# Perceiver decoder: attention weights, contexts and row statistics prepared in the feed-forward's program

## The chip, the cores and the metric

The kernel runs on 1 core of one Trainium2 chip. The metric is the device time of one execution in microseconds (us), as the median of 3 runs. The engines are PE (matrix engine; PEld is its weight load), DVE (vector), ACT (scalar, activation functions), POOL (GpSimd) and SP, which issues the DMA transfers.

## The reference, cut to what matters

Six residual blocks are applied in turn to x (32 batches x 64 positions x 256). The change touches the third and the fourth.

```
x = x + L0_xattn(ctx_1024, layernorm(x), ...)     # program "latent_attention"
x = x + L0_attn(layernorm(x), ...)                # program "linear_feed", linear attention
x = x + L0_ffn(layernorm(x), ...)                 # program "linear_feed", gate/up/down with silu
x = x + L1_xattn(layernorm(x), ctx_1024, ...)     # "decoder": cross attention, 16 heads of 16
x = x + L1_attn(layernorm(x), ...)                # "decoder": gated cell over 64 positions
x = x + L1_ffn(layernorm(x), ...)                 # "decoder": 8 experts, entmax gates

def _L1_xattn_ref(query, key, value, mask, Wq, bq, Wk, bk, Wv, bv, Wo, bo):
    Q, K, V = query @ Wq.T + bq, key @ Wk.T + bk, value @ Wv.T + bv      # split into heads
    energy = where(mask == 0, -1e20, einsum(Q, K) / sqrt(16))
    return (softmax(energy) @ V) @ Wo.T + bo
```

## The kernel before, in words

The 2048 rows of x stay in on-chip memory as `x_sb`, in NT = 16 tiles of 128 rows; NCH = 4 chunks of PER = 4 tiles. Three programs run one after the other. Each is one block in which every engine has its own fixed list of instructions, ordered by hand, and counting semaphores between them; at a program's end (`end_stage`) the semaphores are cleared and all engines meet at a barrier. Nothing crosses that barrier but what lies in memory.

**`linear_feed`** (names `body_...` in the trace). For each chunk c, PE runs five turns i = 0..4 that mix three things: the gate and up products of the chunk before (`gate_up(c-1, i)`), and `contexts`, `states` and `keys_values` of the linear attention of this chunk's tiles. DVE does in a turn `hidden(c-1, i)` (silu times up, line 571), `contexts` (518 to 528), `states` (508, 510), `keys_values` (497, 498) and `y_row` (bn_stats of one tile, 113). At i = 4 comes `norm_y.close`, seven small operations (120 to 128), then POOL's power (137), then `scale_rows`. ACT's next copies of transposed rows (`rows_turned`, line 420), which PE's `queries` (294) wait for, come in its list behind `high(c-1, 5)` (460), which waits for DVE's `hidden(c-1, 5)`. POOL's list is `hidden_low` (line 256, the low part of each hidden block for the three-pass products), with the power for each chunk between hidden_low 3 and 4. `down` (367) waits for all six hidden_low. After chunk 3 there is no next chunk to turn, so PE goes from gate_up(2, 5) straight to `down(2, 0)`. A tail follows: hidden(3, 0..5), with gate_up alone on PE, then down(3, 0..3).

**`decoder`** (names `dec_`, `att_`, `moe_`). Its opening, in front of the loop over the 32 batches, loads the query, key and value weights and the first context (256 keys of 2 batches, transposed, `ctx_raw`), splits weights and context into a high part in fp32r and a low remainder, computes the layer-norm statistics of all 16 tiles (`rows_stats`: four bn_stats and the seven small operations; POOL's power), applies them (`rows_apply`, 140), transposes the rows on PE (`turn_rows`, 901), has ACT copy them out (1106), and multiplies by Wq (`queries`, 910, two products of 128x512 per half). `keys_proj(0)` and `values_proj(0)` are three-pass products (line 83). ACT writes one half of the scaled queries `q_bd` (1112) and DVE the other (1258); the loop's first `energies(0)` (942) waits for the last of them. The first exponentials of the loop are at line 1128.

`TileStats` holds statistics of a norm; `goes_on(stats, rstd, first)` lets a later program go on with tiles that an earlier one began, as `Ahead` does for the linear attention.

```
            turn_rows(0)
            turn_rows(1)
            pe.wait_ge(q_loads, 32)
            queries(0)
            pe.wait_ge(pre, 2)
            keys_proj(0)
            turn_rows(2)
            queries(1)
            values_proj(0)
            turn_rows(3)
            queries(2)
            queries(3)
```

## Time and profile before

| | |
|---|---|
| median of 3 runs | 2220.39 us (2218.87 to 2220.65) |
| the profiled execution | 2218.44 us, its span 2216.6 us |
| PE, PEld busy | 96%, 85% of the span |
| DVE, ACT, POOL busy | 55%, 52%, 23% |
| mean granted PE clock | 0.985 |
| `linear_feed` in the span | about 903 to 1113 us |
| opening of the decoder | 1113.8 us to the first energies at 1151.2 us |

The timeline's times are from the span's start. A row gives start, duration of the group, engine, line, operation, what it writes and reads, the count, and in brackets how long the engine idled before it and what released it.

### The profile page before, as it was taken

The numbers are of one execution on the slowest core, as the hardware profiler recorded it, in microseconds if no ns is written. First come the engines' busy times: TensorE is split into PE (matmuls) and PEld (weight loads), VectorE is DVE, ScalarE is ACT, GpSimd is POOL, SyncE is SP. The second block draws the span as 40 slices with busy tenths as digits, with TensorE's granted clock in tenths as the row PEclk, the third lists the DMA queues.
The fourth block names the chain that finished last, engine by engine and source line by source line (L and its number), as shares of the span: only waits on it lengthen the run. The fifth ranks groups of instructions, "written<-read, shape, count | busy, mean of one in ns | idle before, by whom it ended". The sixth has DMA issues, their size and how long they took to land.

```text
span 2216.6 us, 50712 instructions
## 1 busy us (share of the span) xinstructions
PE 2118.9 (96%) x20881; PEld 1883.0 (85%) x20881; DVE 1218.3 (55%) x3619; ACT 1157.9 (52%) x2620; POOL 502.8 (23%) x416
## 2 busy tenths in 40 slices
PE   6999999999999999699879999999999999999999
PEld 5899999998989998466758878878999999999998
DVE  5656565656555555657556777842874843342411
ACT  4656565656565555333237766653444444444443
POOL 0000011000000000122221221232444444444444
PEclk9999999999999999999989999998999999999999
DMA  4000200000000000000031100010101101011000
GB/s 143 21 16 21 72 21 16 23 15 28 18 18 20 16 6 1 11 1 1 1 116 31 31 26 27 12 40 1 58 1 39 39 1 39 1 39 38 1 10 29
DMA packets 48803, 58.08 MB, mean 26 GB/s; under 512 B 6528, under 2 KB 40128, under 8 KB 48448
## 3 DMA queue, kind: packets, MB, share of 16 engines
q1 hardware_dynamic: 48576, 54.85, 7.8%
q8 instruction: 167, 2.74, 0.5%
q14 instruction: 60, 0.49, 0.1%
HBM read 46.72 MB, written 2.10 MB: 22 GB/s over the span
## 4 chain that ended last, share of the span: by engine, by line
PE 45%; DVE 3%; issue 1%; ACT 1%; POOL 0%; POOLq 0%; DVEq 0%; ACTq 0%
PE bank L83 20%; PE bank L1031 16%; PE bank L969 3%; PE bank L955 2%; PE bank L942 1%; PE bank L910 1%; PE bank L978 1%; PE bank L997 1%; DVE dec_room L140 0%; DVE att_rden L1290 0%; DVE att_vz L1272 0%; PE bank L1002 0%; DVE dec_ts_rawa L113 0%; PE bank L901 0%; PE bank L990 0%
## 5 line engine op out<-in xcount | busy, mean ns | idle before, releaser
L861 POOL TENSOR_TENSOR moe_h<-moe_hr,moe_h 128x512 fp32r<-128x512 f32 x256 | 340.8, 1331 | 431.3 <-ACT moe_hr L1175 431.3
L1174 ACT ACTIVATE moe_h<-bank,dec_b 128x512 fp32r<-128x512 f32 x256 | 176.4, 689 | 401.5 <-PE bank L83 378.0
L83 PE MATMUL bank<-lat_wv,lat_kv_t 128*128 128x256 f32 (+1 forms) x1728 | 261.9, 301 | 8.7 <-DVE lat_wv L2188 4.9
L83 PE MATMUL bank<-lat_kv_t,lat_qk 128*128 128x320 f32 x1536 | 258.8, 317 | 0.0
L83 PEld LDWEIGHTS bank<-lat_wv,lat_kv_t 128*128 128x128 f32 x1728 | 224.4, 190 | 16.8 <-ACT lat_v L2096 5.7
L83 PEld LDWEIGHTS bank<-lat_kv_t,lat_qk 128*128 128x128 f32 x1536 | 225.2, 188 | 8.7
L2121 ACT ACTIVATE lat_p<-bank,lat_neg_max 128x320 f32<-128x320 f32 x256 | 135.2, 528 | 166.2 <-DVE lat_neg_max L2237 166.2
L2231 DVE TENSOR_TENSOR lat_qk<-bank,lat_qk 128x256 fp32r<-128x256 f32 x256 | 96.7, 420 | 197.6 <-ACT lat_qk L2115 197.4
L83 PE MATMUL bank<-dec_xt,dec_lo 128*128 128x512 f32 x512 | 202.5, 396 | 0.0
L2237 DVE TENSOR_REDUCE lat_neg_max<-bank 128x1 f32<-128x320 f32 x256 | 125.7, 492 | 132.3 <-PE bank L83 132.1
L1175 ACT ACTIVATE moe_hr<-bank,dec_b 128x512 f32<-128x512 f32 x256 | 174.6, 682 | 0.0
L1652 POOL TENSOR_TENSOR lat_rs_rstdc<-lat_rs_varc,lat_rs_halfc 128x4 f32<-128x4 f32 x16 | 16.2, 1015 | 692.4 <-DVE lat_rs_varc L1644 692.4
L1031 PE MATMUL bank<-dec_hi,moe_h 128*128 128x256 f32 x1024 | 164.0, 282 | 0.4 <-POOL moe_h L861 0.4
L1031 PE MATMUL bank<-dec_lo,moe_h 128*128 128x256 f32 x1024 | 163.8, 282 | 0.0
L1031 PE MATMUL bank<-moe_hi,moe_h 128*128 128x256 f32 x1024 | 163.2, 282 | 0.4 <-POOL moe_h L861 0.4
L83 PE MATMUL bank<-dec_xt,dec_hi 128*128 128x512 f32 x512 | 162.9, 400 | 0.0
L83 PE MATMUL bank<-dec_xt,moe_hi 128*128 128x512 f32 x512 | 159.4, 392 | 0.0
L1031 PEld LDWEIGHTS bank<-dec_hi,moe_h 128*128 128x128 f32 x1024 | 149.1, 190 | 11.4 <-POOL moe_h L861 0.8
L1128 ACT ACTIVATE att_p<-att_sc,att_low 128x256 f32<-128x256 f32 x256 | 113.2, 510 | 85.6 <-DVE att_low L1282 85.6
L1031 PEld LDWEIGHTS bank<-moe_hi,moe_h 128*128 128x128 f32 x1024 | 148.6, 189 | 10.8 <-POOL moe_h L861 0.6
L1031 PEld LDWEIGHTS bank<-dec_lo,moe_h 128*128 128x128 f32 x1024 | 139.6, 189 | 0.0
L1549 DVE SCALAR_TENSOR_TENSOR x_sb<-bank,moe_xs,x_sb 128x256 f32<-128x256 f32 x96 | 41.3, 473 | 145.2 <-PE bank L1031 145.2
(321 smaller groups left out, 4060.3 us busy)
## 6 DMA issues: line engine op xcount, KB each, us to landing
raw_w<-in_L_ffn_W SPq DMA_DIRECT2D x16, 1024.0 KB, 6.4
lat_ctx_raw<-in_ctx SPq DMA_DIRECT2D x16, 512.0 KB, 4.0
att_ctx_raw<-in_ctx_turned SPq DMA_DIRECT2D x16, 512.0 KB, 3.7
lat_kv_t<-lat_lt SPq DMA_DIRECT2D x32, 128.0 KB, 2.1
out_x<-x_sb SPq DMA_DIRECT2D x4, 512.0 KB, 2.9
x_sb<-in_x SPq DMA_DIRECT2D x1, 1792.0 KB, 14.7
lat_xl_now<-lat_xl SPq DMA_DIRECT2D x7, 256.0 KB, 4.5
ahead_room<-in_L_xattn_Wq SPq DMA_DIRECT2D x1, 1024.0 KB, 7.3
```

Source lines behind the costliest of these rows:

```text
L83: mm = pe.matmul(out, lhs(a, k), rhs(b, k), start=first and k == 0 and n == 0, stop=last and k == KD - 1 and n == 2)
L861: pool.tensor_tensor(h[:, g % 2, 1, :], hr[:, g % 2, :], h[:, g % 2, 0, :].bitcast(F32), ALU.subtract).then_inc(h_lo, 1)
L955: mm = pe.transpose(pt_bank[half][:, (2 * n + t) * P:(2 * n + t + 1) * P], p[:, m, 2 * half + n, t * P:(t + 1) * P], k.ident[:, :])
L969: mm = pe.matmul(o_bank[r * W32:(r + 1) * W32, (2 * what + m) * S:(2 * what + m + 1) * S], of, pt[:, m, r, t, par * S:(par + 1) * S], star ...
L1031: mm = pe.matmul(y_bank[c % 2 * 2 + i // 2][:, i % 2 * D:(i % 2 + 1) * D], h[:, n % 2, b, i * P:(i + 1) * P], w2(e % 2, a)[:, at, :], star ...
L1128: act.activation(p[:, m, r, :], sc[:, m, r, :], ACT.Exp, bias=low[:, m, r:r + 1], scale=-1.0).then_inc(p_ready, 1)
L1174: act.activation(h[:, n % 2, 0, :], h_bank[n % 2][:, :], ACT.Relu, bias=bias).then_inc(h_hi, 1)
L1175: act.activation(hr[:, n % 2, :], h_bank[n % 2][:, :], ACT.Relu, bias=bias).then_inc(h_f, 1)
L1549: dve.scalar_tensor_tensor(out=x_sb[:, t, :], in0=src(t), scalar=xs[:, t, e:e + 1], in1=x_sb[:, t, :], op0=ALU.mult, op1=ALU.add).then_inc ...
L2121: act.activation(p[:, hp % 2, h * LK:(h + 1) * LK], s_bank[h][:, 0:LK], ACT.Exp, bias=neg_max[:, u:u + 1], accum_out=rsum[:, u:u + 1]).the ...
L2231: dve.tensor_tensor(cols(1), bank[:, 0:KD * P].rearrange("p (k b n) -> p k b n", k=KD, b=2), cols(0).bitcast(F32), ALU.subtract).then_inc( ...
L2237: dve.tensor_reduce(neg_max[:, u:u + 1], s_bank[h][:, 0:LK], AX.X, ALU.max, negate=True).then_inc(s_max, 1)
```

## The change

A class `Near` holds, for the cross attention, context buffers, Wq, Wk, Wv, the biases bq and bk and the row statistics in memory that lives from `linear_feed` into the decoder (on the right side of the memory, by `RightSide`; the buffers `h` and `hr` of the experts take that place later). In `linear_feed`, SP issues seven more loads (two biases, three weights, two contexts); DVE splits Wk and Wv (turns (1,1) and (1,2)) and the first context (turns (2,1) and (3,1)), and takes statistics of the finished chunks 0, 1 and 2 (turns (2,2) and (2,3), (3,2) and (3,3), and in the tail after hidden 2 and 3); POOL computes their power. ACT makes a silu on one column in chunk 0, so that its table is loaded there. In the decoder's opening these steps are gone; PE starts with `keys_proj(0)`; ACT starts with an exponential on one column; POOL clears `vz` after the rows of three chunks are applied; a few constants for the gated cell are made after batch 2 of the loop, not ahead of it.

```diff
+class Near:
+    CHUNKS = 3
...
+        self.ctx_raw = sb("ctx_raw", [P, 2, KD, 2 * S2])
+        self.ctx_t = sb("ctx_t", [P, 2, 2, KD, 2 * S2], F32R)
+        self.wq, self.wk, self.wv = sb("wq", [P, KD, D]), sb("wk", [P, 2, KD, D], F32R), sb("wv", [P, 2, KD, D], F32R)
...
 linear_feed, SP:
+                sp.dma_start(near.bq[:, :], column(w["L1_xattn_bq"])).then_inc(near_in, 16)
+                sp.dma_start(near.bk[:, :], column(w["L1_xattn_bk"])).then_inc(near_in, 16)
+            sp.dma_start(near.wq[:, :, :], rows(w["L1_xattn_Wq"])).then_inc(near_in, 16)
+            for g, n in enumerate(("k", "v")):
+                sp.dma_start(kv_raw[:, g], rows(w["L1_xattn_W" + n])).then_inc(near_in, 16)
+            for i in range(2):
+                sp.dma_start(near.ctx_raw[:, i], ...).then_inc(near_in, 16)
 linear_feed, POOL:
+                if c >= 2:
+                    near.norm.power(pool, c - 2)
                 norm_y.power(pool, c)
...
+                if h == 3:
+                    near.norm.power(pool, NCH - 2)
 linear_feed, ACT:
+                    if c == 0 and i == 1:
+                        act.wait_ge(l_xn, 1)
+                        act.activation(table[:, :], xn[:, 0, 0, 0:1], ACT.Silu)
 linear_feed, DVE:
+            def near_split(c, i):
+                if (c, i) == (1, 1):
+                    dve.wait_ge(near_in, 112)
+                    for g, dst in enumerate((near.wk, near.wv)):
+                        dve.tensor_copy(dst[:, 0], kv_raw[:, g]).then_inc(near_hi, 1)
+                if (c, i) == (1, 2):
...
+                        dve.tensor_tensor(dst[:, 1], kv_raw[:, g], dst[:, 0].bitcast(F32), ALU.subtract)...
+                if (c, i) == (2, 1):
+                    dve.tensor_copy(near.ctx_t[:, 0, 0], near.ctx_raw[:, 0]).then_inc(near_hi, 1)
+                if (c, i) == (3, 1):
...
+                    dve.tensor_tensor(near.ctx_t[:, 0, 1], near.ctx_raw[:, 0], ..., ALU.subtract)...
...
+                    if i == 2 and c >= 2:
+                        near_rows(c - 2)
+                    if i == 3 and c >= 2:
+                        near.norm.close(dve, c - 2)
+                    near_split(c, i)
...
+                if h == 2:
+                    near_rows(NCH - 2)
+                if h == 3:
+                    near.norm.close(dve, NCH - 2)
 decoder, PE:
+            keys_proj(0)
             turn_rows(0)
             turn_rows(1)
-            pe.wait_ge(q_loads, 32)
             queries(0)
-            pe.wait_ge(pre, 2)
-            keys_proj(0)
+            values_proj(0)
             turn_rows(2)
             queries(1)
-            values_proj(0)
             turn_rows(3)
 decoder, ACT:
+            act.activation(table[:, :], bk[:, 0:1], ACT.Exp)
+            keys_proj(0)
             rows_turned(0)
-            act.wait_ge(kv_loads, 48)
-            act.copy(wk[:, 0], wkr).then_inc(w_hi, 1)
-            act.copy(wv[:, 0], wvr).then_inc(w_hi, 1)
             rows_turned(1)
             act.wait_ge(pre, 1)
             queries(0)
-            keys_proj(0)
...
-            act.wait_ge(r_const, 5)
             for b in range(B):
+                if b == 4:
+                    act.wait_ge(r_const, 4)
 decoder, DVE:
+            rows_apply(0)
...
-            rows_stats(0)
-            rows_stats(1)
-            rows_apply(0)
-            rows_stats(2)
-            rows_apply(1)
...
-            split_keys(0)
...
+            rows_apply(1)
+            rows_apply(2)
+            rows_stats(3)
             queries(0)
-            rows_stats(3)
-            rows_apply(2)
+            rows_apply(3)
             dve.wait_ge(loads, 96)
-            s.give(dve.tensor_scalar(mask[:, :], mask_i, 0.0, MASKED, ALU.is_equal, ALU.mult))
-            queries(1)
-            rows_apply(3)
             dve.wait_ge(consts, 4)
             values_proj(0)
+            queries(1)
+            s.give(dve.tensor_scalar(mask[:, :], mask_i, 0.0, MASKED, ALU.is_equal, ALU.mult))
             queries(2)
             queries(3)
...
+                if b == 2:
+                    late_constants()
```

PE at the decoder's opening (`rows_a` are the rows and their transposes, `att_ctx_t` or `right_ctx_t` the split context). Before:

```order
L901 MATMUL bank<-ident,rows_a 128x128 x16
L910 MATMUL bank<-rows_a,att_wq 128x512 x4
L83 MATMUL bank<-att_ctx_t,att_wk 128x256 x12
L901 MATMUL bank<-ident,rows_a 128x128 x8
L910 MATMUL bank<-rows_a,att_wq 128x512 x4
L83 MATMUL bank<-att_wv,att_ctx_t 128x256 x12
L901 MATMUL bank<-ident,rows_a 128x128 x8
L910 MATMUL bank<-rows_a,att_wq 128x512 x8
L1061 MATMUL bank<-ident,dec_b1r 128x64
```

PE at the same place in the change:

```order
L83 MATMUL bank<-right_ctx_t,right_wk 128x256 x12
L968 MATMUL bank<-ident,rows_a 128x128 x16
L977 MATMUL bank<-rows_a,right_wq 128x512 x4
L83 MATMUL bank<-right_wv,right_ctx_t 128x256 x12
L968 MATMUL bank<-ident,rows_a 128x128 x8
L977 MATMUL bank<-rows_a,right_wq 128x512 x4
L968 MATMUL bank<-ident,rows_a 128x128 x8
L977 MATMUL bank<-rows_a,right_wq 128x512 x8
L1127 MATMUL bank<-ident,dec_b1r 128x64
```

The matmuls are the same; the key products stand first and the value products one place earlier.

DVE in `linear_feed`, chunk 2, at the end of turn 3 (`body_kvm` and `body_ts_rawy` are the linear attention's own). Before:

```order
L508 TENSOR_TENSOR body_kvm<-bank,body_mask 128x2x128
L510 TENSOR_TENSOR body_kvm<-bank,head_mask 128x2x8
L113 BN_STATS body_ts_rawy<-body_y 128x6
L571 TENSOR_TENSOR body_hf<-body_silu,bank 128x512
L518 TENSOR_SCALAR body_dmax<-bank 128x16
```

DVE at the same place in the change (`right_ts_...near` are the new statistics):

```order
L556 TENSOR_TENSOR body_kvm<-bank,body_mask 128x2x128
L558 TENSOR_TENSOR body_kvm<-bank,head_mask 128x2x8
L113 BN_STATS body_ts_rawy<-body_y 128x6
L120 TENSOR_TENSOR right_ts_tmpnear<-right_ts_rawnear 128x4
L121 TENSOR_TENSOR right_ts_tmpnear<-right_ts_rawnear 128x4
L122 TENSOR_TENSOR right_ts_tmpnear<-right_ts_rawnear 128x4
L124 TENSOR_SCALAR right_ts_meannear<-right_ts_tmpnear 128x4
L125 TENSOR_TENSOR right_ts_tmpnear<-right_ts_tmpnear 128x4
L126 TENSOR_SCALAR right_ts_tmpnear<-right_ts_tmpnear 128x4
L128 SCALAR_TENSOR_TENSOR right_ts_varnear<-right_ts_tmpnear 128x4
L619 TENSOR_TENSOR body_hf<-body_silu,bank 128x512
```

Seven small operations stand now ahead of hidden of turn 4; in the same way the four bn_stats stand at the end of turn 2, ahead of hidden of turn 3.

## Rows read from the trace of the kernel before

**Rows 1.** The page, part 1: busy us, share of the span, instructions
```profile
PE 2118.9 (96%) x20881; PEld 1883.0 (85%) x20881; DVE 1218.3 (55%) x3619; ACT 1157.9 (52%) x2620; POOL 502.8 (23%) x416
```

**Rows 2.** Timeline of the decoder's opening, 1113 to 1157 us
```profile
1113.97 1.40 DVE L113 BATCH_NORM_STATS2 dec_ts_rawa<-x_sb 128x6 f32<-128x256 f32 x4
...
1118.39 1.38 DVE L140 TENSOR_SCALAR rows_a<-x_sb,dec_ts_meana,dec_ts_rstda 128x256 f32<-128x256 f32 x4
...
1118.85 1.97 PE L901 MATMUL bank<-ident,rows_a 128*128 128x128 f32 x8 [6.70 <-DVE rows_a L140]
1119.58 1.65 ACT L1106 COPY rows_a<-bank 128x256 f32<-128x256 f32 x4 [19.26 <-PE bank L901]
...
1124.11 4.63 PE L910 MATMUL bank<-rows_a,att_wq 128*128 128x512 f32 x8
...
1141.05 1.41 PE L901 MATMUL bank<-ident,rows_a 128*128 128x128 f32 x8 [0.52 <-DVE rows_a L140]
...
1142.30 7.21 PE L910 MATMUL bank<-rows_a,att_wq 128*128 128x512 f32 x16
...
1151.18 1.15 PE L942 MATMUL bank<-att_kt,q_bd 32*128 32x256 f32 x16 [1.47 <-DVE q_bd L1258]
...
1152.26 1.70 PE L83 MATMUL bank<-att_ctx_t,att_wk 128*128 128x256 f32 x12
...
1152.90 1.28 ACT L1128 ACT_TABLE_LOAD   x1 [2.84 <-DVE att_low L1282]
...
1155.16 1.46 PE L955 MATMUL bank<-ident,att_p 128*128 128x128 f32 x8 [1.20 <-ACT att_p L1128]
```

**Rows 3.** Stretches (us): busy PE, PEld, DVE, ACT, POOL (count), PE clock, DMA share, GB/s
```profile
1113.70:1151.20 37.50, 26.11 (x93) 15.24 (x93) 24.31 (x81) 13.89 (x30) 10.48 (x13) 0.82 0.52 155
1116.00:1126.00 10.00, 5.62 (x19) 4.12 (x20) 9.68 (x38) 4.12 (x10) 5.01 (x5) 0.50 0.80 240
...
1020.00:1040.00 20.00, 18.41 (x113) 14.76 (x112) 13.58 (x39) 7.15 (x13) 7.16 (x6) 1.00 0.01 2
```

**Rows 4.** Stretches, same columns, behind an idle PE: in the decoder's loop
```profile
1157.00:1161.00 4.00, 4.00 (x80) 3.68 (x82) 0.76 (x2) 2.19 (x6) 1.51 (x2) 0.58 0.34 80
...
1307.00:1311.00 4.00, 4.00 (x28) 3.15 (x28) 2.20 (x14) 1.21 (x3) 0.00 (x0) 0.57 0.48 135
```

**Rows 5.** Timeline at 1306 us: what the second of these stretches follows
```profile
1306.03 1.10 PE L978 MATMUL bank<-att_wo,att_ot 128*128 128x256 f32 x4 [1.97 <-DVE att_vz L1272]
```

**Rows 6.** Timeline of `linear_feed`, chunk 2 (y row additions, hidden, next queries)
```profile
1008.45 0.69 DVE L571 TENSOR_TENSOR body_hf<-body_silu,bank 128x512 f32<-128x512 f32 x1 [0.38 <-PE bank L83]
...
1014.38 0.69 DVE L571 TENSOR_TENSOR body_hf<-body_silu,bank 128x512 f32<-128x512 f32 x1 [1.14 <-ACT body_silu L453]
...
1015.80 1.30 POOL L256 TENSOR_TENSOR body_ht<-body_hf,body_ht 128x512 fp32r<-128x512 f32 x1 [4.67 <-ACT body_ht L460]
1016.00 1.38 DVE L528 TENSOR_TENSOR body_y<-body_ctxn,body_xn 128x256 f32<-128x256 f32 x1
...
1018.64 0.69 DVE L571 TENSOR_TENSOR body_hf<-body_silu,bank 128x512 f32<-128x512 f32 x1
...
1020.26 0.43 DVE L528 TENSOR_TENSOR body_y<-body_ctxn,body_xn 128x256 f32<-128x256 f32 x1
...
1022.22 0.69 DVE L571 TENSOR_TENSOR body_hf<-body_silu,bank 128x512 f32<-128x512 f32 x1 [0.18 <-PE bank L83]
...
1024.59 3.70 PE L294 MATMUL bank<-body_xt,ahead_wq 128*128 128x512 f32 x8 [1.59 <-ACT body_xt L420]
```

**Rows 7.** Timeline of `linear_feed`, end of chunk 3
```profile
1071.03 8.21 PE L367 MATMUL bank<-body_wd,body_ht 128*128 128x256 f32 x54 [3.80 <-POOL body_ht L256]
```

**Rows 8.** Timeline: the feed-forward's low parts, the silu table, a cast of the context
```profile
906.01 3.42 DVE L583 TENSOR_TENSOR body_wgu<-ahead_room,body_wgu 128x1536 fp32r<-128x1536 f32 x2
...
945.54 1.28 ACT L453 ACT_TABLE_LOAD   x1
...
1123.78 0.69 DVE L1243 CAST att_ctx_t<-att_ctx_raw 128x1024 fp32r<-128x1024 f32 x1
```

More of the change, by code:

```diff
@@ L205, in linear_feed @@
         ht = tools.sb("ht", [P, 2, NH, CH], F32R)
+        kv_raw = tools.sb("kv_raw", [P, 2, KD, D])
+        table = tools.sb("table", [P, 1])
+        near = k.near
+        near.norm.goes_on(sem("near_stats"), sem("near_rstd"), 0)
         loads, consts = sem("loads"), sem("consts")
+        near_in, near_hi, near_lo = sem("near_in"), sem("near_hi"), sem("near_lo")
         l_shift, f_shift, l_xn, l_psum, l_xt = sem("l_shift"), sem("f_shift"), sem("l_xn"), sem("l_psum"), sem("l_xt")
@@ L228, in _ @@
             sp.dma_start(beta[:, :], everywhere(w["L0_attn_beta"])).then_inc(loads, 16)
+            with nc.allow_non_contiguous_dma(reason="biases as columns"):
+                sp.dma_start(near.bq[:, :], column(w["L1_xattn_bq"])).then_inc(near_in, 16)
[4 more added lines that the diff above has]
+            for i in range(2):
+                sp.dma_start(near.ctx_raw[:, i], rows(w["ctx_turned"])[:, :, i * 2 * S2:(i + 1) * 2 * S2]).then_inc(near_in, 16)
             sp.wait_ge(loads, 64)
+            sp.wait_ge(near_in, 112)
         @block.gpsimd
         def _(pool):
-            for norm in (norm_y, norm_f):
+            for norm in (norm_y, norm_f, near.norm):
                 norm.setup(pool, consts)
@@ L697, in decoder @@
             ot = att.sb("ot", [P, 2, KD, P])
-            wkr, wvr = (sc[:, m].rearrange("p r n -> p (r n)")[:, 0:KD * D].rearrange("p (k n) -> p k n", k=KD) for m in range(2))
             mask_i = p[:, 0, 0, :].bitcast(I32)
+            k.near_room.close()
         moe = Tools(nc, ctx, "moe")
-        h = moe.sb("h", [P, 2, 2, CH], F32R)
-        hr = moe.sb("hr", [P, 2, CH])
+        right = RightSide(nc, ctx)
+        h = right.sb("h", [P, 2, 2, CH], F32R)
+        hr = right.sb("hr", [P, 2, CH])
         acc = moe.sb("acc", [P, NT, D])
@@ L862, in low_half @@
                                    ALU.subtract).then_inc(h_lo, 1)
-            for c in range(NCH - 1):
-                norm_a.power(pool, c)
-            split_keys(0)
             norm_a.power(pool, NCH - 1)
@@ L2373, in perceiver @@
             k.ahead = Ahead(nc, inner)
-            for stage in STAGES:
-                STAGE_BODIES[stage](nc, k, x_sb, banks, w)
-                k.end_stage()
+            latent_attention(nc, k, x_sb, banks, w)
+            k.end_stage()
+            k.near_room = ctx.enter_context(ExitStack())
+            k.near = Near(nc, k.near_room)
+            linear_feed(nc, k, x_sb, banks, w)
+            k.end_stage()
         decoder(nc, k, x_sb, banks, w, out)
```

98 lines of the change are left out of this document (52 added, 46 removed).

## The prediction

> **What bounds the kernel now.** I read the page first: PE is busy for 96% of the span and DVE for 55% [rows 1], so what PE does not wait for costs nothing. The places where PE does wait are few, and two of them are the stages that the change touches.
>
> The first is the decoder's opening, in the timeline. PE's first matmul stands behind an idle stretch of 6.70 us, which DVE's statistics, POOL's power and the first normalised row end (bn_stats at 1113.97, application at 1118.39, transposes at 1118.85 [rows 2]). From 1113.7 to the first energies at 1151.2 PE is busy for 26.11 of 37.5 us, and of the granted clock only 0.82 is left; from 1116 to 1126 it is 0.50, the lower level of 1.2 GHz, after that idle stretch [rows 3]. At the end the loop's first exponential waits for a table load of 1.28 us that starts only when its input is there, and PE idles 1.20 us for it [rows 2].
>
> The second is the feed-forward's program. In its turns PE is saturated (18.41 of 20 us busy at full clock from 1020 to 1040 [rows 3]), but DVE has little air: ahead of the hidden product it idles 0.38 us in turn 2 and 1.14 us in turn 3 of chunk 2, nothing in turn 4, and 0.18 us before the last one [rows 6]. That last one is on PE's path: ACT's copies stand behind it, and PE idles 1.59 us for them before the queries [rows 6]. At the end of chunk 3 PE idles 3.80 us for POOL's low parts [rows 7], which stand in POOL's list behind the power of statistics that DVE closes at the end of the same turns.
>
> **The change, part by part.**
>
> *Opening, PE.* What is left are the same matmuls, in a chain that starts at once, since keys and the rows of three chunks have nothing to wait for but DVE's application (four tiles in 1.38 us). At full clock, from 1113.8: keys_proj 1.70; four tiles turned 1.41; the next four paced by ACT's copies of the first four, 1.65 and some 0.35 of waits, 2.0; queries(0) half of 7.21, 3.6; values_proj 1.70; turn_rows(2) 1.41; queries(1) 3.6 [rows 2]. That is 15.4 us. Behind it comes the same tail as before, from turn_rows(3) at 1141.05 to the energies at 1151.18, 10.1 us [rows 2]. Sum 25.5, energies at 1139.3. The tail's bias transpose waits for the late loads; SP issues them behind fewer transfers than before, so they are no later.
>
> *Opening, clock.* PE idles from 1112.15, where it last worked (6.70 us before 1118.85 [rows 2]), to 1113.8, is busy 3 us, then half idle for 2. Before, an idle stretch of 1.97 us in the loop [rows 5] was followed by 4 us at 0.57 [rows 4], while 1.59 us [rows 6] was followed by none (1.00 from 1020 to 1040 [rows 3]). This case lies between them. Bounds: no loss, or the first queries at 4.63 instead of 3.6 and the transposes at 1.97 instead of 1.41 [rows 2], some 2.5 us with the key and value products. I take 1.5, since the low stretch ends in both loop places after about 4 us and part of it falls on a paced stretch. Energies at 1140.8: **10.4 us gained**.
>
> *Statistics, splits and casts off the opening* are in this number; the remaining DVE list (12 tiles applied, statistics of chunk 3: 4.1 and 2.2 us) runs under the 25 us of matmuls. So does POOL's clear of `vz`, now behind twelve rows.
>
> *Exponential's table.* It moves to the start of ACT's list, in front of the key copy, which PE's 1.70 us product releases only after it. PE's idle 1.20 us goes [rows 2]: **1.2 us**. The Trainium skill, page "ScalarE: Activation LUTs", section "Terms", gives about 2.7 us for a load; its section on what the load costs gives 1283 ns. The trace agrees with the second, and by the first this term would be larger by 1.4 us.
>
> *Clock behind it.* The stretch at 0.58 from 1157 to 1161 [rows 4] follows two waits, 1.47 and 1.20 us [rows 2]. With the second gone, only one like the harmless 1.59 is left. At most 0.42 of 4 us, 1.7 us, come back; at least nothing. I take **1.0**.
>
> *Silu's table* was loaded under a wait of ACT (1.28 us at 945.54 [rows 8]; the gate product came later). Moved into chunk 0 it lies in ACT's idle time too: 0. The seven more loads start at 903 us and are waited for first in turn (1,1), behind the silu table's row at 945.54 [rows 8]: 0.
>
> *Feed-forward, chunk 1.* Two casts of 512 cost half each of the 0.69 of a cast of 1024 [rows 8], 0.7 together, and fit before hidden. Two subtractions: 3.42 for two of 1536 [rows 8] gives 0.6 each, 1.2 against an idle time like the 1.14: some 0.1 late, and the 0.18 before the last hidden takes it. 0.
>
> *Chunk 2.* The cast of 0.69 against 0.38: 0.3 late. Four bn_stats, 1.4 by their row [rows 2] and 1.3 where they follow one another, against 1.14: 0.5 late. Seven small operations: two rounds of statistics lie between 1113.97 and 1118.39 in the opening, 2.2 each [rows 2], so they take 0.9 beside 1.3 of bn_stats, and there is only 0.16 of air before turn 4's hidden (0.69 at 1018.64, no idle [rows 6]): 1.2 late. This reaches norm_y's close and the last hidden, which has 0.18 to give: ACT's copies and PE's queries **1.0 us** later. PE's idle stretch becomes 2.6 us, beyond the 1.97 that was followed by a fall, so I count one: 0.43 of 4 us, **1.7 us**. Bounds 0 and 1.7.
>
> *Chunk 3.* The subtraction of 1024, 1.1 by the same rate, fits 1.14; bn_stats 0.2 late; the small ones bring it to 0.9. POOL's power, the low parts and `down` follow: the 3.80 us [rows 7] become 4.7, **0.9 us**. POOL's additional power lies in its own idle time before norm_y's. The clock falls there already.
>
> *Tail.* Statistics of chunk 2 lie in DVE's idle time between hidden products, where PE computes gate and up alone: 0.
>
> *Port of DVE and POOL.* The addition of two tiles took 1.38 us while POOL's low part ran and 0.43 without [rows 6]. The new subtractions have two inputs in on-chip memory too, but stand where POOL waits for the next high part (idle 4.67 us before its row), so I add nothing. If all three met POOL, it would be 0.95 each, 2.9 in all. The Trainium skill, page "SBUF — State Buffer", section "Who interferes with whom", says that a DVE instruction with two SBUF inputs and a GpSimd one that reads SBUF exclude each other, the later one waiting for the whole of the other. By that rule the trace's 0.95 are a wait; it speaks against moving subtractions beside POOL's work, and would cost here up to what the row gives.
>
> **The sum.** Gained 10.4 + 1.2 + 1.0 = 12.6; lost 1.0 + 1.7 + 0.9 = 3.6; net 9.0 less. The profiled execution took 2218.44 us, so 2209.4 by it. It is 2 us below the median 2220.39 of the runs; against the median I forecast **2211.4 us**.
>
> **The rivals.**
>
> *A, the clock holds* (0.20). PE sees no fall in the opening nor in chunk 2, and gets back the whole of the one at 1157: gained 11.9 + 1.2 + 1.7, lost 1.9, net 12.9: 2207.5. For it: 1.59 us passed; against: 1.97 did not.
>
> *B, the clock falls wherever it can* (0.20). The opening loses 2.5 instead of 1.5, the one at 1157 stays, and chunk 1, whose queries wait nearly as long, falls as well: gained 9.4 + 1.2, lost 3.6 + 1.7, net 5.3: 2215.1. For it: 0.1 us more is enough if chunk 1 stands at the edge.
>
> *C, the opening does not shrink* (0.05). Something that I take as hidden, such as the late loads or the constants, holds the tail where it was. Then only 1.2 is gained against 3.6: 2222.8. Against it: those loads are issued earlier than before.
>
> *D, DVE becomes the bound of the feed-forward* (0.05), which would make it slower than before. If the idle times before hidden cannot be used, because a late kvm or kpre stops PE's contexts and states, all the new DVE work in the turns counts: 2 x 2.2 of statistics, 1.4 of casts, 2.3 of subtractions, 8.1, with 2.9 of the port, and a fall of the clock at three boundaries, 5.1. That is 16.1 against 12.6, net +3.5; with the tail's 2.2 it is +5.7, 2226. It decides from 12.6 us lost. Against it: PE is at 18.41 of 20 us in a stretch of such turns [rows 3], so what DVE gives it there comes early enough, and a DVE that is late by a microsecond first eats that lead.
>
> **How the numbers follow.** The forecast has 0.50. A measurement here tells about 0.2%, 4.4 us, from no change: faster is below 2216.0, slower above 2224.8. Faster: 0.50, A's 0.20 and 0.12 of B's; same: B's rest and C, 0.13; slower: D, 0.05. The range goes from just beyond A (2206.5) to beyond B, where the unknown waits of the opening add up (2217.5).
>
> **What would show it.** Right: energies at some 27 us behind the barrier instead of 37.4; the first PE row 0.1 us behind it; the exp table load at the start of ACT's list; PE's idle before queries of chunk 3 (now 1.59) at 2.6 and half clock behind it; 4.7 instead of 3.80 before the last but one `down`. Wrong: waits of contexts or states on DVE in the turns; an opening in which PE waits for ACT's copies all through (four engines' semaphores take more than the 0.35 that I gave); a subtraction that takes 1.5 us or more.

## The result, and the profile after

| | before | after |
|---|---|---|
| median of 4 runs each, us | 2220.47 (2218.87 to 2220.65) | 2199.99 (2197.96 to 2201.67) |
| profiled execution, us | 2218.44 | 2199.23 |
| its span, us | 2216.6 | 2196.9 |

The ratio is 0.9912, 95% interval 0.9899 to 0.9926: faster by 20.5 us. The forecast was 9.0 us less, 2211.4, with a range down to 2206.5. The direction was right and the size was not: the result lies outside the range.

First the page of the changed kernel, its span and busy times, which answer to [rows 1]:

```profile
span 2196.9 us, 50710 instructions
...
PE 2108.5 (96%) x20881; PEld 1873.2 (85%) x20881; DVE 1218.9 (55%) x3622; ACT 1155.9 (53%) x2620; POOL 499.9 (23%) x414
```

PE has the same 20881 instructions and is busy 10.4 us less (before 2118.9). Work that only moved can't do that. About half of the 19.7 us of span was idle time; the other half is the same matmuls running faster.

The timeline of the decoder's opening after the change, which answers to [rows 2]:

```profile
1116.90 1.28 ACT L1250 ACT_TABLE_LOAD   x1 [12.04 <-PEq L2416]
1116.94 1.66 PE L83 MATMUL bank<-right_ctx_t,right_wk 128*128 128x256 f32 x12 [1.73 <-PEq L2416]
...
1118.44 1.03 PE L968 MATMUL bank<-ident,rows_a 128*128 128x128 f32 x8
...
1119.37 2.29 ACT L1172 COPY rows_a<-bank 128x256 f32<-128x256 f32 x8
1119.89 1.23 PE L968 MATMUL bank<-ident,rows_a 128*128 128x128 f32 x8 [0.41 <-DVE rows_a L140]
1120.96 3.60 PE L977 MATMUL bank<-rows_a,right_wq 128*128 128x512 f32 x8
...
1123.99 2.00 PE L83 MATMUL bank<-right_wv,right_ctx_t 128*128 128x256 f32 x12
...
1130.13 1.04 PE L968 MATMUL bank<-ident,rows_a 128*128 128x128 f32 x8
...
1139.89 1.15 PE L1010 MATMUL bank<-att_kt,q_bd 32*128 32x256 f32 x16 [1.47 <-DVE q_bd L1325]
...
1142.53 1.45 PE L1023 MATMUL bank<-ident,att_p 128*128 128x128 f32 x8
```

PE starts at once and idles only 1.73 us at the change of programs. The energies stand 22.95 us behind its first matmul; before they stood 37.4 us behind the same point. The transposes of the first exponentials follow without the idle 1.20 us of [rows 2].

The same stretches as in [rows 3, 4], of the changed kernel (columns as there; the last but two is PE's clock):

```profile
1116.90:1139.90 23.00, 21.08 (x91) 12.25 (x92) 15.09 (x43) 13.02 (x30) 3.28 (x7) 1.00 0.56 161
1157.00:1161.00 4.00, 4.00 (x91) 3.77 (x90) 2.65 (x15) 3.84 (x10) 0.00 (x0) 1.00 0.02 4
985.00:1030.00 45.00, 42.72 (x248) 31.56 (x247) 33.95 (x107) 15.81 (x30) 14.89 (x13) 1.00 0.00 1
```

The clock is full in the opening (0.82 before), at the loop's start (0.58 before), and through the feed-forward's chunk 2, where I had counted a fall.

The waits of PE in the feed-forward's program, at the ends of chunks 1, 2 and 3; before they were 1.59, 1.59 [rows 6] and 3.80 us [rows 7]:

```profile
981.80 3.70 PE L339 MATMUL bank<-body_xt,ahead_wq 128*128 128x512 f32 x8 [1.77 <-ACT body_xt L465]
...
1027.60 3.70 PE L339 MATMUL bank<-body_xt,ahead_wq 128*128 128x512 f32 x8 [2.28 <-ACT body_xt L465]
...
1074.74 9.32 PE L412 MATMUL bank<-body_wd,body_ht 128*128 128x256 f32 x54 [4.49 <-POOL body_ht L297]
```

Set against each other by stages, the spans differ by 19.7 us: the opening 14.4 less; the loop 2.8 less (1.2 for the table's wait, 1.7 for the clock at its start); the feed-forward's program 2.2 more; the program ahead of it 0.9 more (a low stretch of the clock at 49 us, which the profile of the kernel before has not and those of all twelve kernels below have, with or without the change); and the expert stage, of which the change touches nothing but where its buffers lie in memory, **5.6 less**. No step of the prediction is there.

Where it lies can be seen in PE's clock. Between 1520 and 1550 us, first the kernel before, where PE is at work for all of it, then the changed one:

```profile
1520.00:1550.00 30.00, 30.00 (x170) 27.27 (x170) 5.05 (x17) 7.30 (x12) 6.51 (x7) 0.77 0.00 1
```

```profile
1520.00:1550.00 30.00, 29.53 (x195) 26.96 (x193) 10.25 (x6) 12.29 (x20) 13.82 (x8) 0.93 0.00 1
```

The clock falls there although PE doesn't idle. Microsecond by microsecond, the low stretches are 3.4 us long, or that twice or three times, and cost 1.7 us for each 3.4, since the granted clock is 0.50 in them. Before there is 13.7 us of low time in the expert stage (1525 to 1546), after 6.8 us; the last microseconds of the span, low in every profile, are left out here and below. What PE does ahead of a fall, in its timeline of the changed kernel:

```profile
1514.85 2.74 PE L83 MATMUL bank<-dec_wrs,dec_xt 128*128 128x8 f32 x24
1517.45 1.07 PE L83 MATMUL bank<-dec_xt,dec_hi 128*128 128x512 f32 x2
1518.32 0.63 PE L83 MATMUL bank<-dec_xt,dec_lo 128*128 128x512 f32 x1
```

The router's 24 matmuls of 128x8 stand in a row, 2.6 us, and behind them two matmuls of 128x512 take 1.07 us instead of 0.62. Before, there is four times 3.4 us of it, after twice: 3.4 of the 5.6 us. The other 2.2 are spread over 256 steps, and the second line of experiments is about them.

### The profile page after: what moved, and what is told of

Same layout as the page of the kernel before. It is cut to its first block, busy times and chain, and to the rows that moved or that the text cites. A ratio compares the mean times of both kernels' runs of the same rounds, so it can differ in the third digit from the quotient of the medians.

```text
span 2196.9 us, 50710 instructions
## 1 busy us (share of the span) xinstructions
PE 2108.5 (96%) x20881; PEld 1873.2 (85%) x20881; DVE 1218.9 (55%) x3622; ACT 1155.9 (53%) x2620; POOL 499.9 (23%) x414
## 4 chain that ended last, share of the span: by engine, by line
PE 45%; DVE 3%; issue 1%; ACT 1%; POOL 0%; POOLq 0%; DVEq 0%; ACTq 0%
PE bank L83 20%; PE bank L1099 16%; PE bank L1037 3%; PE bank L1023 2%; PE bank L1010 1%; PE bank L1046 1%; PE bank L977 1%; PE bank L1065 1%; DVE att_rden L1357 0%; DVE dec_room L140 0%; PE bank L1070 0%; DVE att_vz L1339 0%; DVE att_sc L1349 0%; DVE right_ctx_t L1309 0%; PE bank L1058 0%
## 5 line engine op out<-in xcount | busy, mean ns | idle before, releaser
L931 POOL TENSOR_TENSOR right_h<-right_hr,right_h 128x512 fp32r<-128x512 f32 x256 | 341.5, 1334 | 424.9 <-ACT right_hr L1241 424.9
L1240 ACT ACTIVATE right_h<-bank,dec_b 128x512 fp32r<-128x512 f32 x256 | 176.5, 690 | 396.4 <-PE bank L83 370.5
L1241 ACT ACTIVATE right_hr<-bank,dec_b 128x512 f32<-128x512 f32 x256 | 174.5, 681 | 0.0
L1099 PE MATMUL bank<-dec_hi,right_h 128*128 128x256 f32 x1024 | 162.3, 280 | 0.5 <-POOL right_h L931 0.5
L1099 PE MATMUL bank<-dec_lo,right_h 128*128 128x256 f32 x1024 | 162.3, 280 | 0.0
L1099 PE MATMUL bank<-moe_hi,right_h 128*128 128x256 f32 x1024 | 161.9, 280 | 0.4 <-POOL right_h L931 0.4
L1099 PEld LDWEIGHTS bank<-dec_hi,right_h 128*128 128x128 f32 x1024 | 147.9, 189 | 11.1 <-POOL right_h L931 0.9
L1099 PEld LDWEIGHTS bank<-moe_hi,right_h 128*128 128x128 f32 x1024 | 147.1, 188 | 11.7 <-POOL right_h L931 0.6
L1099 PEld LDWEIGHTS bank<-dec_lo,right_h 128*128 128x128 f32 x1024 | 138.4, 188 | 0.0
```

The costliest lines, as they stand in the source:

```text
L931: pool.tensor_tensor(h[:, g % 2, 1, :], hr[:, g % 2, :], h[:, g % 2, 0, :].bitcast(F32), ALU.subtract).then_inc(h_lo, 1)
L1099: mm = pe.matmul(y_bank[c % 2 * 2 + i // 2][:, i % 2 * D:(i % 2 + 1) * D], h[:, n % 2, b, i * P:(i + 1) * P], w2(e % 2, a)[:, at, :], star ...
L1240: act.activation(h[:, n % 2, 0, :], h_bank[n % 2][:, :], ACT.Relu, bias=bias).then_inc(h_hi, 1)
L1241: act.activation(hr[:, n % 2, :], h_bank[n % 2][:, :], ACT.Relu, bias=bias).then_inc(h_f, 1)
```

## The experiments

"Stage time" below is from ACT's first relu of an expert to that of the next, 32 steps. "Low time" is the time at the lower clock in the profile, stretch by stretch.

**1. The router's blocks.** In two kernels, one made from the kernel before and one from the changed kernel, the router's 16 tiles go one by one behind the expert steps; the last two stand together behind step 26, so there twelve narrow matmuls are left in a row:

```
-                if n in (17, 18, 19, 26):
-                    router((17, 18, 19, 26).index(n))
+ROUTER_STEP = list(range(11, 23)) + [24, 25, 26, 26]
...
+                for t in range(NT):
+                    if ROUTER_STEP[t] == n:
+                        router(t)
```

> The kernel before, with the router's 16 tiles of six 128x8 matmuls each done one behind each expert step (steps 11 to 22 and 24 to 26) instead of 24 matmuls in a row behind steps 17, 18, 19 and 26. The matmuls are the same. Theory 'the blocks of narrow matmuls make the clock fall': the four low stretches of 3.4 us between 1525 and 1546 (6.8 us lost) vanish, time about 2213.6. Rival 'the falls belong to something else, or the narrow matmuls are as bad one tile at a time': still three or four low stretches, 2220.4.

> The changed kernel with the same spread router. Its profile has two low stretches there instead of four. Theory 'the blocks of narrow matmuls make the clock fall': both vanish, 3.4 us, about 2196.6, and the spread kernels differ from each other by 3.4 us less than before and after do (17 instead of 20.5), because the number of falls at the blocks was what differed. Rival 'the change gained those 3.4 us by something of its own': 2200 stays, or the two spread kernels still differ by 20.5.

Measured: before_router_spread 2212.63 us (ratio to the kernel before 0.9965, 0.9954 to 0.9977), 7.4 less than the kernel before beside it (2220.07). After_router_spread 2194.13 us (ratio 0.9887, 0.9874 to 0.9900). The stretch from 1520 to 1550, first of before_router_spread, then of after_router_spread:

```profile
1520.00:1550.00 30.00, 30.00 (x201) 26.92 (x201) 7.78 (x20) 11.50 (x19) 11.29 (x9) 1.00 0.00 1
```

```profile
1520.00:1550.00 30.00, 30.00 (x211) 27.76 (x210) 15.29 (x25) 13.54 (x22) 11.47 (x9) 1.00 0.00 1
```

The router's tiles in after_router_spread now stand between wide matmuls:

```profile
1518.67 0.73 PE L83 MATMUL bank<-dec_wrs,dec_xt 128*128 128x8 f32 x6
1519.26 0.71 PE L83 MATMUL bank<-dec_xt,dec_hi 128*128 128x512 f32 x2
```

No low stretch is left in the expert stage of either, nor in the two later kernels with this edit. The blocks of narrow matmuls made the clock fall. The number of falls is a matter of chance in the changed kernel as in the one before: counted by 3.4 us of low time each, the profiles of the ten kernels that keep the blocks have 4, 3, 1 and 5 (without the change) and 2, 3, 6, 4, 2 and 6 (with it). Executions of one kernel differ as well: the twelve of before_right_pad, below, reach from 2211.48 us, at a mean clock of 0.989, to 2224.30 us at 0.984. After_router_spread gained 5.9 us where 3.4 was expected from the falls in one profile. With the router's falls out of the way, the change is worth 18.5 us, not 20.5, where the expectation had 17; the intervals of the two ratios, some 0.13% or 3 us to each side, are too wide to say how much of the 20.5 was luck with the falls.

**2. The place of the buffers.** In the kernel before, h and hr (and the two context buffers, whose place they take) go to the right end of the memory, with and without padding in their old place:

```
-        h = moe.sb("h", [P, 2, 2, CH], F32R)
-        hr = moe.sb("hr", [P, 2, CH])
+        h = ctx.enter_context(nc.sbuf_tensor("right_h", [P, 2, 2, CH], F32R, side="right"))
+        hr = ctx.enter_context(nc.sbuf_tensor("right_hr", [P, 2, CH], F32, side="right"))
+        pad = moe.sb("pad", [P, 3, 2, CH])       # before_right_pad only
```

> The kernel before, with the hidden products h and hr of the expert stage at the right end of the on-chip memory, as the change has them (over the contexts' buffers, which go to the right end with them), and 12 KB of padding in their old place, so that acc, hi1 and b2 stay where they were. Nothing else differs. Of the 5.7 us that the change gained in the expert stage, about 2.3 lie in the output products (282 ns each before, 280 after, some 0.475 against 0.455 us per four). Theory 'the place of h': that part comes with the address of h, so the output products go to 280 ns and the time to about 2218.1. Rival 'not the place': products stay at 282 ns, time stays at 2220.4 within 0.5.

> As before_right_pad, without the padding, so that acc, hi1 and b2 start 12 KB further down, as they do in the change. Theory 'the place of h': same as with padding, 2218.1. Rival 'the place of the weights hi1 or of acc': only this one gains the 2.3 us, 2218.1 here and 2220.4 with padding. Rival 'not the place': both 2220.4.

Measured: 2217.60 us with padding (ratio 0.9999, 0.9985 to 1.0012) and 2220.56 without (1.0006, 0.9995 to 1.0017): no gain in either that is clear of noise, and the output products take 281 to 284 ns by the pages (282 before, 280 in the change). So the theory 'the place of h' fell as it was put, though the 2217.60 lies near its 2218.1; that median stands between two groups of executions, 2211.5 to 2214.8 and 2220.4 to 2224.3 us. Nor did 'not the place' hold, because the stage times said more than the mean: the kernel before takes 90.0 us for an odd expert and 89.0 for an even one, both these kernels 89.8 and 90.2, the changed one 89.6 and 89.0. So the place of h does matter, it made the even experts slower, 12 KB more or less for acc and hi1 did nothing, and something else in the change had taken that loss back and more. The one other difference in that stage is that the statistics of `norm_a` no longer lie ahead of the weights: xt, lo0, hi0 and lo1, and behind them acc and hi1, lie 960 bytes lower. Two kernels on that, of which the second leaves acc and hi1 where they were:

```
+        pad = tools.sb("pad", [P, 240])          # after_shifted_960: ahead of norm_r
...
-        norm_a = TileStats(tools, sem("a_stats"), sem("a_rstd"), "a")
...
         br = tools.sb("br", [P, E])
+        norm_a = TileStats(tools, sem("a_stats"), sem("a_rstd"), "a")   # before_shifted_960
```

> The changed kernel with 960 bytes of padding ahead of the decoder's buffers: as much as the statistics of norm_a took there before the change moved them to the right end. All the decoder's buffers at the left (xt, lo0, hi0, lo1, hi1, acc) are then at the addresses of before_right; instructions are the same. Time of 32 expert steps, from ACT's first relu of each expert, odd experts and even experts: before 90.0 and 89.0 us, before_right 89.8 and 90.23, the change 89.6 and 89.0. Theory 'the expert products' pace depends on where the weights lie in the on-chip memory': with the padding they take before_right's 89.8 and 90.23, the time 5 us more, about 2205. Rival 'the pace comes with something else in the change': 89.6 and 89.0 stay, 2200.0.

> The kernel before with norm_a's 960 bytes allocated behind the decoder's other buffers instead of ahead of them: xt, lo0, hi0 and lo1 lie 960 bytes lower, as in the change, while h, hr, acc and hi1 stay at their places on the left. Instructions are the same. Theory 'only the place of the weights counts': odd and even experts take the change's 89.6 and 89.0 us (before 90.0 and 89.0), 1.6 us less. Theory 'it is the weights' place against that of h': another pair of numbers, since h is not where the change has it. Rival 'no place counts' has fallen with after_shifted_960. The time itself scatters more than this by the falls of the clock, so the expert times decide.

ACT's relus that open experts 2, 3 and 4 (so first an even, then an odd expert between them), in the timelines, first of the changed kernel, then of after_shifted_960:

```profile
1655.38 0.69 ACT L1240 ACTIVATE right_h<-bank,dec_b 128x512 fp32r<-128x512 f32 x1 [1.53 <-PE bank L83]
...
1744.38 0.69 ACT L1240 ACTIVATE right_h<-bank,dec_b 128x512 fp32r<-128x512 f32 x1 [1.54 <-PE bank L83]
...
1833.97 0.69 ACT L1240 ACTIVATE right_h<-bank,dec_b 128x512 fp32r<-128x512 f32 x1 [1.53 <-PE bank L83]
```

```profile
1657.98 0.69 ACT L1241 ACTIVATE right_h<-bank,dec_b 128x512 fp32r<-128x512 f32 x1 [1.54 <-PE bank L83]
...
1748.21 0.69 ACT L1241 ACTIVATE right_h<-bank,dec_b 128x512 fp32r<-128x512 f32 x1 [1.55 <-PE bank L83]
...
1838.01 0.69 ACT L1241 ACTIVATE right_h<-bank,dec_b 128x512 fp32r<-128x512 f32 x1 [1.54 <-PE bank L83]
```

89.0 and 89.6 us, against 90.2 and 89.8: with 960 bytes of padding and the same instructions, before_right's pair comes back exactly, so the two moves (h to the right, weights 960 bytes down) make up the whole way from the pair before to the pair after. The median is 2206.14 us, 6.1 us above the changed kernel's (expected 5; one more stretch of low clock at the router is in its profile). In before_shifted_960 the pair is 89.8 (odd) and 90.0 (even), a fourth pair, with h still at the left; its median is 2221.14 (ratio 1.0011, 1.0002 to 1.0019). So it isn't the weights' place alone but theirs together with that of h. The last test of it moves hi1, and of the other buffers only what lies behind it (b2 and the gates' small ones), in the kernel after_spread_and_chunk_end of experiment 4:

```
         acc = moe.sb("acc", [P, NT, D])
+        pad = moe.sb("pad", [P, 240])
         hi1 = moe.sb("hi1", [P, 2, KD * F], F32R)
```

> The kernel of after_spread_and_chunk_end with 960 bytes of padding ahead of hi1 (the high parts of the odd experts' weights), so that hi1 alone lies where it lay before the change. Theory of the place: even experts, which use hi0 and lo0, keep 89.0 us; odd experts change from 89.6, to between 89.0 and 90.2, in all between 2.4 us less and 2.4 us more. Rival 'a shift of hi1 does nothing' (12 KB did nothing): odd ones stay at 89.6.

Measured: odd experts 90.36 us instead of 89.60, even ones 89.02 instead of 89.0; 2195.68 us against 2192.94 beside it. Its relus at the same places:

```profile
1649.63 0.69 ACT L1248 ACTIVATE right_h<-bank,dec_b 128x512 fp32r<-128x512 f32 x1 [1.54 <-PE bank L83]
...
1738.65 0.69 ACT L1248 ACTIVATE right_h<-bank,dec_b 128x512 fp32r<-128x512 f32 x1 [1.54 <-PE bank L83]
...
1829.01 0.69 ACT L1248 ACTIVATE right_h<-bank,dec_b 128x512 fp32r<-128x512 f32 x1 [1.54 <-PE bank L83]
```

Only the experts whose weights moved changed, by 0.76 us of 89.6. What in the memory makes the pace depend on the place stays open; that it does, and that the odd experts' 90.0 and 89.6 us before and after lie in it, is shown. Over the four odd experts that is 1.6 of the 2.2 us; the rest lies in the first expert's steps, among side work, and wasn't traced further.

**3. The exponential's table.** The small exponential that the change put at the head of ACT's list is taken away; then, in a second kernel, the late constants and ACT's wait for them also go back ahead of the loop:

```
-            act.activation(table[:, :], bk[:, 0:1], ACT.Exp)
...
-                if b == 4:
-                    act.wait_ge(r_const, 4)
```

> The changed kernel without the small exponential at the head of ACT's list, so that the table load comes before the loop's first exponential again. Theory of the prediction: 1.2 us later, PE idles 1.20 us behind the energies, and this second wait brings back the clock's fall at the loop's start (1.7 us): 2202.9. Rival 'the fall needed the half-clock opening before it, not the second wait': 1.2 us only, 2201.2, no low stretch within 15 us of the energies.

> The changed kernel without the small exponential, and with ACT's wait for the late constants (r_const) back ahead of the loop, and DVE's three late constants too. In after_no_exp_table the load had run at 1139.75, ahead of the energies, and the energies-to-transposes time stayed at 2.64 us. Theory 'what put the load on the path was the second wait: the load stands between the wait for r_const and the wait for the energies' masking': here it starts only when DVE's low value is there, PE idles about 1.2 us between keys_proj(1) and the first transposes (3.9 us from energies), all later points 1.2 us later. Rival 'the load had been early because PE came earlier': it stays at about 1139.8 and the 2.64 us too.

The first, in its timeline:

```profile
1139.75 1.28 ACT L1194 ACT_TABLE_LOAD   x1
1140.84 1.15 PE L1010 MATMUL bank<-att_kt,q_bd 32*128 32x256 f32 x16 [1.46 <-DVE q_bd L1324]
...
1143.48 1.45 PE L1023 MATMUL bank<-ident,att_p 128*128 128x128 f32 x8
```

The load runs ahead of the energies, and from these to the transposes it is 2.64 us, as in the changed kernel (1139.89 to 1142.53). The small exponential is worth nothing. The median of 2202.63 us lies near the theory's 2202.9 by luck: neither the 1.20 us of idle time nor a fall behind the energies came, so theory and rival were both wrong. What makes the time longer in the profile are four stretches of low clock at the router instead of two and one in chunk 2, none of it where the edit is. The second kernel, in its timeline and in the stretch behind (line 1537 makes the last of the constants that ACT waits for):

```profile
1140.54 1.15 PE L1010 MATMUL bank<-att_kt,q_bd 32*128 32x256 f32 x16 [1.47 <-DVE q_bd L1323]
1140.56 0.14 DVE L1537 TENSOR_SCALAR dec_o_bias<-dec_gate_bias 128x1 f32<-128x1 f32 x1
...
1142.27 1.28 ACT L1194 ACT_TABLE_LOAD   x1 [2.84 <-DVE att_low L1347]
...
1144.52 1.46 PE L1023 MATMUL bank<-ident,att_p 128*128 128x128 f32 x8 [1.22 <-ACT att_p L1194]
```

```profile
1146.00:1150.00 4.00, 3.96 (x72) 3.74 (x76) 0.76 (x2) 2.55 (x6) 1.87 (x2) 0.57 0.21 47
```

Now the load waits for DVE's low value, PE idles 1.22 us, and the clock falls behind it: all as before the change. With two waits ahead of the exponential (constants, low value) the load comes behind them; with one it comes ahead of it. The constants themselves are not late: the last is made by 1140.70, 1.6 us before the load starts. So the 1.2 us belong to the wait for `r_const`, which the change moved to b = 4. The median is 2208.57 us (2200.16 to 2209.27), 5.9 more than without this step; 1.3 and 1.7 us of that are the step itself, and its profile has six stretches at the router instead of four (3.4 us).

Over all profiles, the fall behind the energies came in 4 of the 6 kernels that have the second wait, and in none of the 8 without it. It doesn't need a half-clock opening ahead of it, as the rival of the first run had it: after_no_exp_table_wait_first has the fall behind an opening at full clock, and after_stats_in_opening, whose opening has half clock for 6.8 us, has none.

**4. The statistics.** Once their place in the feed-forward's turns, once the opening itself:

```
-                    if i == 2 and c >= 2:
-                        near_rows(c - 2)
-                    if i == 3 and c >= 2:
-                        near.norm.close(dve, c - 2)
...
                 if c >= 1:
                     residual(c - 1, 3)
+                if c >= 2:
+                    near_rows(c - 2)
+                    near.norm.close(dve, c - 2)
```

> The changed kernel with the four bn_stats and seven small operations of chunks 0 and 1 moved from the turns of chunks 2 and 3 to the end of DVE's chunk, behind the last residual, where DVE idles 2.38 us for PE before its next hidden product; POOL's powers follow one step behind. Theory 'the turns' idle time was too small for them': PE's gap before the queries of chunk 3 goes from 2.29 us back to about 1.7, the one at the end of chunk 3 from 4.49 to about 3.8, together 1.3 less, 2198.7. Rival 'they cost nothing in the turns, the gaps moved for another reason (the splits)': gaps and time stay. Either way it is within what the falls of the clock scatter, so the gaps decide.

```
-        norm_a.goes_on(sem("a_stats"), sem("a_rstd"), Near.CHUNKS)
+        norm_a.goes_on(sem("a_stats"), sem("a_rstd"), 0)
...
+            rows_stats(0)
+            rows_stats(1)
             rows_apply(0)
+            rows_stats(2)
```

> The changed kernel with the statistics of chunks 0 to 2 taken back to the decoder's opening (weights, contexts, biases and table stay in the feed-forward's program): PE starts with keys_proj(0) at once, but the first transposes wait for eight bn_stats, two rounds of small operations and POOL's power. Theory 'the statistics stood on the opening's path': first transposes about 5 us behind the start instead of 1.5, 3.5 us later, the clock falls behind that wait (up to 2.9 us), feed-forward 1.3 us shorter; net about 5 us, 2205. Rival 'keys and queries hide the statistics': within 1 us of 2200.

The third kernel has the spread router of experiment 1 and the statistics at the chunk's end together:

> The changed kernel with the spread router and the statistics at the end of the chunk together. Gaps alone give 1.3 us against after_router_spread's 2194.1. Theory: the gaps count in full once no fall of the clock behind the router blurs them: 2192.8. Rival: the shorter gap lets the fall at 1104 in (it was there in after_stats_at_chunk_end and not in the change, 1.7 us), then 2194.5 and the statistics' place is worth nothing.

In after_stats_at_chunk_end the two gaps are what they were before the change:

```profile
1027.15 3.70 PE L341 MATMUL bank<-body_xt,ahead_wq 128*128 128x512 f32 x8 [1.58 <-ACT body_xt L467]
...
1073.57 8.20 PE L414 MATMUL bank<-body_wd,body_ht 128*128 128x256 f32 x54 [3.78 <-POOL body_ht L297]
```

So the statistics alone, not the splits, had made them longer, by 0.7 us each. Yet the median is 2204.15 us, above the changed kernel's 2199.99: its profile has six stretches of low clock at the router's blocks instead of two, 6.8 us (one run of its five took 2196.40). Why these came isn't shown; chance is enough, as experiment 1 has it. With the router spread, after_spread_and_chunk_end takes 2192.94 us (ratio to the kernel before 0.9883, 0.9870 to 0.9896), 1.2 less than after_router_spread against 1.3 expected. That agreement isn't proof, since the two were measured against different executions of the kernel before and the intervals overlap; and the fall that its rival named did come (3.4 us from 1105.5 in its profile), while those of after_router_spread at 1024.6 and 1290.9 are gone and a new one stands at 931.4. The gaps decide, and they are back to 1.58 and 3.78 us. It has the lowest median of all kernels here, 25.8 us below the kernel before beside it (2218.70).

After_stats_in_opening takes 2204.87 us, as expected (2205), but with other terms: the first transposes stand 4.88 us behind PE's first matmul instead of 1.50, and a second wait of 2.58 us follows.

```profile
1119.91 1.78 PE L958 MATMUL bank<-ident,rows_a 128*128 128x128 f32 x8 [3.22 <-DVE rows_a L140]
...
1124.27 1.97 PE L958 MATMUL bank<-ident,rows_a 128*128 128x128 f32 x8 [2.58 <-DVE rows_a L140]
...
1145.53 1.15 PE L1000 MATMUL bank<-att_kt,q_bd 32*128 32x256 f32 x16 [1.46 <-DVE q_bd L1314]
```

The energies come 30.5 us behind the first matmul instead of 22.95, 7.6 us later; PE is busy 2.1 us longer for the same matmuls, because the clock is low again between 1120 and 1128 (0.57). Of the opening's 14.4 us, then, the statistics brought 7.6; the weights, contexts and constants together with PE's order the other 6.8, which no run took apart further.

## Why the prediction was wrong, step by step

The steps as the prediction put them, with what they measured, in us (minus is time gained).

| step | forecast | measured |
|---|---|---|
| opening, PE's chain (25.5 behind the start) | -11.9 | -14.4, with 22.95 |
| opening, clock | +1.5 | 0 |
| exponential's table | -1.2 | -1.2, by another part of the change |
| clock behind it | -1.0 | -1.7 |
| chunks 1, 2 and 3, gaps | 0, +1.0, +0.9 | +0.2, +0.7, +0.7 |
| clock in chunk 2 | +1.7 | 0 in the profiled run |
| the rest of the feed-forward, and the program ahead (one more low stretch in each, at 930 and 49 us) | 0 | +1.5 |
| expert stage | not considered | -5.6 |
| sum | -9.0 | -19.8 (by the spans -19.7) |

**The step that failed** is the first inference of the prediction, "what PE does not wait for costs nothing", by which the expert stage has no term at all; it measured -5.6 us, with PE busy throughout, 3.4 of it in falls of the clock at the router and 2.2 by the place of the buffers. It is half of the 10.7 us that are missing. Most of the rest lies in two terms that were there and mis-sized: the opening's chain by 2.5 us and its clock by 1.5, and the fall counted for chunk 2 is 1.7 more. The prediction took the clock to fall behind idle stretches only, and all its rows lie around the stages that the change touches. The page of the kernel before has PE's clock in forty slices of 55 us:

```profile
PEclk9999999999999999999989999998999999999999
```

The first 8 is the opening, which the prediction priced; the second, the 28th slice from 1496 us, is the router, which it passed over. After the change both are 9. A table of stretches over the whole span would have shown the falls at 1525 to 1546 under a PE that is busy throughout. Even so, their number could not have been forecast: it was 1 to 6 over ten kernels, so the 3.4 us of this pair of profiles were luck. The range could have been widened by it, by some 5 us to both sides; 2199.99 would still have lain just outside.

**The opening's chain** was right in its order and in what paces it, and 2.5 us too long. I added the durations of groups, 3.6 for half the queries and 1.41 for four tiles turned, though a group's row lasts until its last matmul has ended and the next group begins before. From start to start the queries take 3.03 (1120.96 to 1123.99) and 3.43 us, keys 1.50. And 1.41 was the duration of a group that followed DVE's tiles; in the changed kernel such a group takes 1.03. The largest error is in the eight tiles that are turned first: 3.4 us in the forecast (1.41 and 2.0), 2.52 in the trace (1118.44 to 1120.96), a wait of 0.41 included. That ACT's copies pace the second four, as forecast, can't be read from the bracket, which names DVE; but ACT's first copy ends at 1119.74, behind DVE's row at 1119.51, and the transposes then follow ACT's copies at 0.27 us a tile. The tail, which I took from start to start, came out at 9.76 against 10.1 us.

**The opening's clock** was a choice between two rows, 1.59 us of idle time without a fall and 1.97 with one. PE idles 1.73 us here, and none of the eight kernels that begin with the keys and keep the statistics out of the opening has a fall there. "No loss", one end of the bounds, was the value, and rival A was right on this point.

**The fall in chunk 2** was right as a mechanism and is a matter of chance: with the gap of 2.28 us it came in 3 of 5 kernels (after_router_spread, and both without the table's exponential), with 1.59 in none of 9. In the profile of the changed kernel it did not come.

**The table** was right in its amount by luck. I read that the load "starts only when its input is there" and took the small exponential for the cure; the cure was the wait that moved (experiment 3).

**DVE's new work** in the feed-forward was nearly right: near's bn_stats and small operations cost 0.7 where I had 1.0 and 0.9, and the subtraction of 1024 took 1.20 us where I had 1.1. The two subtractions of 512 took 0.67 and 0.68, beside no instruction of POOL, so the 2.9 us for the port did not arise. The sentence of the Trainium skill, page "SBUF — State Buffer", section "Who interferes with whom", on a DVE instruction with two inputs in on-chip memory and POOL excluding each other was therefore put to no test by the changed kernel: no new subtraction meets one of POOL's. The opening of the kernel before bears on it: of two equal subtractions of 512 (lines 1462 and 1463) the first took 0.69 us and the second, during POOL's of the context, 1.75 us. Of the Trainium skill's page "ScalarE: Activation LUTs" all profiles here agree with the 1283 ns of "What ACT_TABLE_LOAD costs" (1.28 us each) and not with the 2.7 us of "Terms". By the section on the cost, the larger figure includes a drain of some 1380 ns; no row here shows one: in the kernel before, the exponential starts at 1154.20, 0.02 us behind the load's end.

Rival A was nearest in its conditions: no fall in the opening, none in chunk 2 of the profile, and the whole of the one at 1157 back. It still forecast 2207.5, for want of the expert stage and by the opening's chain. Rivals B, C and D fell: no wait of contexts or states on DVE appeared, and the opening shrank by more than forecast.

## What to carry to other kernels

Before pricing a change, list every stretch of the whole span in which the granted clock is below full, not only those at the change: such stretches come behind runs of very narrow matmuls on a busy PE too, their number differed from 1 to 6 between the profiles of kernels that differ little ahead of them, and they hide or fake gains of several us. Interleaving the narrow ones with wide ones was worth 7.4 us in the kernel before, some 6 in the changed one, and made every later comparison cleaner. Add up a chain of matmuls from start to start, never by the durations of groups. And when an edit has several parts, take each away alone: the part that was made for the table did nothing, the wait that was moved in passing did it all.

## What the runs showed of the hardware

- The granted clock falls with PE 100% busy: at blocks of 24 matmuls of 128x8 in a row (2.6 us) it fell in every one of the ten profiles at least once; with six of them at a time between wide ones, and once twelve, never in four.
- 960 bytes in the place of the weights against the hidden products change the time of 32 identical steps by up to 1.2 us of 90 (89.0 to 90.2); a shift of acc, hi1 and b2 by 12 KB changed nothing. Five arrangements gave for odd and even experts 90.0 and 89.0, 89.8 and 90.2, 89.6 and 89.0, 89.8 and 90.0, 90.4 and 89.0.
- With one semaphore wait ahead of the activation the table load ran early (1139.75; the activation's input came at 1142.5). With a second wait it ran behind both (1142.27), though the second wait's semaphore had been ready for 1.6 us.
